# The last group of a scan-and-FFN kernel packed to 64 partitions and 256 columns, its gating named as an item of its own, and new slots for the work between scan steps

## The reference

```python
p = patches(x)                                   # (32, 196, 768)
y = layernorm(p, ln1_g, ln1_b) @ W + bias
h = concat([layernorm(y, ln2_g, ln2_b), txt])    # (32, 273, 256)

u = layernorm(h)[:, ::2]                         # every second token
u = u * rsqrt(mean(u * u) + eps) * g_norm
x, gate = split(u @ w_in.T + b_in)               # 256 each
def step(s, xt):                                 # s: (32, 256, 64)
    s = tanh(s * A + xt[:, :, None] * Bm)
    return s, s @ Cm.sum(0) + Dv * xt
out = scan(step, 0, x) * silu(gate)
h = h + repeat(out @ w_out.T + b_out, 2)[:, :273]

f = layernorm(h)
return h + (silu(f @ wg.T) * (f @ wu.T)) @ wd.T  # hidden 768, weights whole numbers / 127
```

## Time and profile before

| | |
|---|---|
| median of 3 runs | 1384.4 us (1383.81 to 1384.44) |
| profiled execution, own time | 1382.85 us |
| its span, first to last instruction | 1381.1 us |
| mean granted TensorE clock | 0.977 |
| busy PE / DVE / ACT / POOL | 1198.4 / 1089.9 / 989.5 / 430.9 us |
| scan slots | 1096 |

### The profile page before, as it was taken

How to read it: one execution, slowest core, us unless ns; L and a number is a source line. 1 busy time by engine, 2 the same in 40 slices (tenths; PEclk the granted TensorE clock), 3 DMA queues, 4 the chain that set the end, 5 groups by cost and what they waited for, 6 DMA issues and landing times.

```text
span 1381.1 us, 25884 instructions
## 1 busy us (share of the span) xinstructions
PE 1198.4 (87%) x7137; PEld 637.7 (46%) x7137; DVE 1089.9 (79%) x2423; ACT 989.5 (72%) x1944; POOL 430.9 (31%) x435
## 2 busy tenths in 40 slices
PE   4587889898989898989898989898999999998866
PEld 3343445354545454545454545454444444443433
DVE  4896878788888888788888788868888888887732
ACT  2367686868686868686868787878778888886632
POOL 6512151515151515151525151524121221221130
PEclk9689999999999999999999999999999999999997
DMA  7412323232323232323131414121323323323200
GB/s 161 126 36 62 74 61 87 61 85 61 85 61 85 61 85 61 85 58 88 53 93 49 97 45 101 40 67 49 100 68 86 86 67 87 85 51 84 55 20 15
DMA packets 154813, 99.59 MB, mean 72 GB/s; under 512 B 129072, under 2 KB 143536, under 8 KB 153424
## 3 DMA queue, kind: packets, MB, share of 16 engines
q1 hardware_dynamic: 151120, 97.58, 27.6%
q10 hardware_dynamic: 3648, 1.46, 0.5%
HBM read 58.39 MB, written 40.60 MB: 72 GB/s over the span
## 4 chain that ended last, share of the span: by engine, by line
PE 31%; issue 27%; ACT 10%; DVE 10%; POOL 9%; DMA 8%; SPq 4%; POOLq 0%; ACTq 0%; DVEq 0%
PE Y L1354 6%; PE U L1344 6%; PE P L1521 5%; PE P L1522 5%; ACT h L1076 4%; DVE U L814 4%; PE P L1455 3%; DMA yT<-y_scr 3%; ACT rawn L1092 3%; DMA y_scr<-y_fx 2%; DMA raw<-in_x 2%; SPq L688 1%; POOL yT L1238 1%; DVE raw_st L821 1%; POOL zT L1242 1%
## 5 line engine op out<-in xcount | busy, mean ns | idle before, releaser
L814 DVE TENSOR_TENSOR U<-h,a_col 128x512 f32<-128x512 f32 x1096 | 707.0, 689 | 128.5 <-ACT h L1076 125.5
L1076 ACT ACTIVATE h<-U 128x512 f32<-128x512 f32 x1096 | 605.8, 607 | 189.0 <-PE U L1344 188.2
L1344 PE MATMUL U<-x_diag,b_st 128*128 128x512 f16 x1096 | 369.3, 385 | 72.8 <-DVE U L814 64.3
L1354 PE MATMUL Y<-h,read_st 128*32 128x512 f32 x2192 | 265.6, 602 | 1.5 <-ACT h L1076 1.5
L1344 PEld LDWEIGHTS U<-x_diag,b_st 128*128 128x128 f16 x1096 | 103.7, 98 | 261.6 <-DVE U L814 182.0
L1279 POOL TENSOR_TENSOR xT_act<-act,xT_act 128x448 f16<-128x448 f32 x114 | 116.6, 1039 | 215.0 <-ACT xT_act L1173 215.0
L1420 PE MATMUL P<-tok_w,xT_act 128*112 128x256 f32 x648 | 159.5, 386 | 1.2 <-ACT xT_act L1100 0.9
L1420 PEld LDWEIGHTS P<-tok_w,xT_act 128*112 128x112 f32 x648 | 113.2, 178 | 42.6 <-issue 10.7
L1536 PE MATMUL P<-down_w,xT_act 128*112 128x256 bf16 x480 | 115.6, 279 | 5.4 <-POOL xT_act L1279 3.0
L1354 PEld LDWEIGHTS Y<-h,read_st 128*32 128x32 f32 x2192 | 57.5, 109 | 129.7 <-issue 120.1
L1537 PE MATMUL P<-down_w,xT_act 128*112 128x256 bf16 x480 | 114.7, 277 | 0.0
(11 more groups left out here) (159 smaller groups left out, 1441.6 us busy)
## 6 DMA issues: line engine op xcount, KB each, us to landing
raw<-in_x SPq DMA_DIRECT2D x42, 448.0 KB, 6.3
gate_scr<-gate_o SPq DMA_DIRECT2D x20, 448.0 KB, 2.5
gate_in<-gate_scr SPq DMA_DIRECT2D x20, 448.0 KB, 3.5
tok_scr<-tok SPq DMA_DIRECT2D x19, 448.0 KB, 3.1
res<-tok_scr SPq DMA_DIRECT2D x19, 448.0 KB, 3.8
out<-res SPq DMA_DIRECT2D x76, 112.0 KB, 5.1
x_diag<-scan_scr SPq DMA_DIRECT2D x312, 16.0 KB
x_diag<-scan_scr SPq DMA_DIRECT2D x304, 12.0 KB
```

The costliest lines, as they stand in the source:

```text
L814: dve.tensor_tensor(U[bank_of(slot)][:, :].rearrange("p (l b) -> p l b", b=B), h[:, (slot - CHUNKS) % RING, :].rearrange("p (l b) -> p l b ...
L1076: sc.activation(h[:, slot % RING, :], U[bank_of(slot)][:, :], ACT.Tanh, scale=1.0 / U_SCALE).then_inc(squashed, 1)
L1344: pe.matmul(U[bank_of(slot)][:, :], b_st[:, c, :], x_diag[:, c, :, t * B:t * B + B], start=False, stop=True, skip_group_check=True).then_i ...
L1354: mm = pe.matmul(Y[c4 * 32:c4 * 32 + 32, :], read_st[:, t, half, :], h[:, (t * CHUNKS + half * RG + c4) % RING, :], start=(t == 0 and half ...
```

## The change

1. Every table of `PLANS` and all of `POOL_ORDER` but "zero" have new numbers.
2. A function `rows_of(group)` gives 64 partitions (16 images x 4 steps) for the last group and 112 for the others. The attention's output, the turn of the FFN's input, its copies, FFN, silu, product, high and low parts, shrink and finish of the last group work on 64 partitions, 64 or 256 columns. Its x and gate copies are 128 columns where they were 224; the loads of its text tokens and its stores step over 4 where they stepped over 7.
3. The gating of the last group, an item of stage "tail", is now `gating_next` at the end of stage "last".

```diff
 PLANS = {
     "image": dict(
-        shrink=(2, 3, 3, 3, 5, 7, 7, 7), turn=(7, 9, 10, 12, 13, 14, 15, 15), attend=(17, 18), average=(20, 22),
-        embed=(19, 19, 19, 20, 20, 21, 24, 25, 26, 29, 29, 29), turn_fx=(30, 30), ffn_gate=(34, 37, 39, 45, 46, 48),
-        ffn_up=(34, 37, 44, 45, 49, 53), turn_xa=(36,), project=(39, 41, 46, 46), finish=(8, 10), raw_patch=(18, 18,
-        18, 18, 18, 18, 19, 19, 20, 22, 22, 22, 22, 22), raw_means=(23,), raw_deviation=(24,), raw_variance=(25,),
-        res_stats=(25,), res_variance=(26,), res_shift=(28,), fx_low_part=(34, 34), tok_stats=(29, 33),
...
-        ffn_silu=(34, 37, 42, 43, 45, 51), act_high_part=(40, 41, 43, 46, 48, 54), normalise=(55, 55, 55, 55, 55,
-        55, 55), residual=(23,)),
+        shrink=(1, 3, 3, 3, 4, 4, 5, 8), turn=(8, 10, 10, 12, 13, 15, 15, 16), attend=(17, 17), average=(20, 21),
+        embed=(18, 18, 18, 19, 20, 22, 24, 24, 24, 26, 29, 29), turn_fx=(30, 30), ffn_gate=(34, 37, 40, 44, 45, 47),
+        ffn_up=(34, 38, 43, 44, 49, 52), turn_xa=(36,), project=(40, 42, 46, 46), finish=(6, 10), raw_patch=(18, 18,
+        18, 18, 18, 19, 20, 20, 20, 20, 20, 20, 20, 20), raw_means=(21,), raw_deviation=(23,), raw_variance=(24,),
+        res_stats=(24,), res_variance=(24,), res_shift=(26,), fx_low_part=(34, 34), tok_stats=(27, 33),
...
+        ffn_silu=(33, 37, 41, 43, 44, 48), act_high_part=(37, 43, 44, 49, 49, 53), normalise=(52, 55, 55, 55, 55,
+        55, 55), residual=(20,)),
     "text": dict(
...
-        ffn_up=(37, 39, 46, 47, 48, 52), turn_xa=(27,), project=(30, 30, 31, 32), finish=(11, 21), res_stats=(30,),
-        res_variance=(31,), res_shift=(31,), fx_low_part=(36, 36), ln_stats=(22,), ln_shift=(25,), x_low_part=(33,),
...
+        ffn_up=(38, 39, 42, 46, 50, 52), turn_xa=(26,), project=(29, 30, 31, 31), finish=(14, 19), res_stats=(30,),
+        res_variance=(30,), res_shift=(31,), fx_low_part=(36, 36), ln_stats=(23,), ln_shift=(25,), x_low_part=(32,),
...
     "last": dict(
...
-        ffn_up=(42, 44, 48, 51, 55, 55), finish=(11, 16), res_stats=(27,), res_variance=(33,), res_shift=(38,),
-        fx_low_part=(46, 50), ffn_product=(55, 55, 55, 55, 55, 55), y_copy=(0,), fx_apply=(35, 38, 46, 48),
...
-        residual=(26,), y_next=(54,)),
...
+        ffn_up=(42, 46, 47, 50, 52, 55), finish=(19, 20), res_stats=(33,), res_variance=(37,), res_shift=(51,),
+        fx_low_part=(55, 55), ffn_product=(55, 55, 55, 55, 55, 55), y_copy=(6,), fx_apply=(32, 34, 35, 36),
...
+        residual=(33,), y_next=(49,)),
...
 POOL_ORDER = {
...
     "last": (
-        ("gating", 0), ("res_rsqrt", 0), ("act_low_part", 0), ("act_low_part", 1), ("act_low_part", 2),
-        ("act_low_part", 3), ("act_low_part", 4), ("skip_term", 0), ("act_low_part", 5)),
+        ("gating", 0), ("res_rsqrt", 0), ("act_low_part", 0), ("act_low_part", 1), ("skip_term", 0),
+        ("act_low_part", 2), ("act_low_part", 3), ("act_low_part", 4), ("act_low_part", 5), ("gating_next", 0)),
...
     "tail": (
-        ("gating", 0), ("res_rsqrt", 0)),
+        ("res_rsqrt", 0),),
...
+        def rows_of(group):
+
+            return 16 * LAST_STEPS if isinstance(group, int) and group == GROUPS - 1 else PT
...
             def ffn_product(k):
                 dve.wait_ge(ffn_u_ps, q * HB + k + 1)
                 dve.wait_ge(fsg_done, q * HB + k + 1)
-                dve.scalar_tensor_tensor(act[:, k, :], fsg[:, k % 2, :], ACT_SCALE * DEQUANT, up_bank(k, scan)[:, 0:4 * PT],
+                n = 4 * rows_of(q)
+                dve.scalar_tensor_tensor(act[:, k, 0:n], fsg[:, k % 2, 0:n], ACT_SCALE * DEQUANT, up_bank(k, scan)[:, 0:n],
                                          ALU.mult, ALU.mult).then_inc(act_done, 1)
...
-            def gating():
+            def gating(q):
...
-                gp.tensor_tensor(zT[:, :, :].rearrange("p k (b t) -> p k t b", t=STEPS),
-                                 y, gate_i[:, 1, :, :].rearrange("p k (t b) -> p k t b", b=B), ALU.mult).then_inc(z_done, 1)
+                n = rows_of(q) // 16
+                gp.tensor_tensor(zT[:, :, 0:B * n].rearrange("p k (b t) -> p k t b", t=n), y[:, :, 0:n, :],
+                                 gate_i[:, 1, :, 0:n * B].rearrange("p k (t b) -> p k t b", b=B), ALU.mult).then_inc(z_done, 1)
...
                 if post and name == "gating":
-                    gating()
+                    gating(q)
+                if post and name == "gating_next":
+                    gating(q + 1)
...
+                m = rows_of(q)
                 for j in range(DB):
-                    mm = pe.matmul(P[0][0:PT, k * D:k * D + D], zT[:, j, k * PT:k * PT + PT], out_w[:, j, :],
+                    mm = pe.matmul(P[0][0:m, k * D:k * D + D], zT[:, j, k * m:k * m + m], out_w[:, j, :],
...
-                bank = P[k // 2][0:PT, (k % 2) * D:(k % 2) * D + D]
+                m = rows_of(d)
+                bank = P[k // 2][0:m, (k % 2) * D:(k % 2) * D + D]
                 for f in range(f0, f0 + 3):
...
                         half = whole_part(down_w[:, f, :])
-                        pe.matmul(bank, act_hi[:, f, k * PT:k * PT + PT], half, start=(f == 0), stop=False)
-                        mm = pe.matmul(bank, act_lo[:, f, k * PT:k * PT + PT], half, start=False, stop=(f == HB - 1))
+                        pe.matmul(bank, act_hi[:, f, k * m:k * m + m], half, start=(f == 0), stop=False)
+                        mm = pe.matmul(bank, act_lo[:, f, k * m:k * m + m], half, start=False, stop=(f == HB - 1))
```

144 lines of the change are left out of this document (80 added, 64 removed).

## The result

The changed kernel takes 1377.28 us (median of 20 executions, 1372.27 to 1381.17), the kernel before 1385.06 beside it (20 executions, 1377.2 to 1388.89): a ratio of 0.9943, with a 95% interval of 0.9931 to 0.9955. It is faster, by 7.8 us where 15 to 16 were forecast; the time lies inside the range, the gain is half. The profiled execution has a span of 1376.0 us, 5.1 under that of the kernel before.

The account below looks back on a forecast made before the run. PE bounds the kernel on average (87% busy), with DVE saturated in part of the image stage and one chain at the end. Terms +1.6 + 0.4 - 6.0 - 3.6 - 7.9 = -15.5 us gave 1369 us as a median, range 1359 to 1382.

Parts of the forecast that it names:

- A: Start, up to the first drive: second half of normalised tokens computed later, first drive near 67.5; +1.6 us.
- B: First scanned stage: moved low part, spread bias splits, last POOL normalisation behind the skip term, delaying a raw load; +0.4 us.
- C: Twelve image stages: PE's 0.58 and ACT's 1.05 us waits vanish, second average costs 0.8; -0.5 us each, -6.0.
- D: Six text stages: residual variance directly follows its statistics, POOL's root runs under grow 30; -0.6 us each, -3.6.
- E: Last scan and the end: residual moved out of the scan and smaller last-group work; -7.9 us in all.
- e3: Last group, first turn to first FFN matmul: fewer columns shorten the rows on the chain; -1.1 us.
- e4: Last group's 48 FFN matmuls at 256 columns, lower clock for the first 5.6 us: 8.0 instead of 12.8; -4.8 us.
- e5: Last product with high and low part at 256 columns: 1.3 instead of 2.32 us; -1.0 us.
- e1: Last scan: residual and its statistics move behind the last grow, ACT's first apply starts sooner; -1.0 us.
- The steady stages do not move: Rival: image and text stages gain nothing because removed waits return as waits for saturated DVE; 1378.5 us, chance 0.20.
- the clock stays down: Rival: lower clock throughout last-group FFN and shrink, 5.4 us more, 1374.4; 1 in 10 of the forecast's chance.
- POOL's chain: Rival: later skip term delays gate's store and load, y's store and raw pixels, bounding the stage; 1393 us, chance 0.12.

Follow-up runs that it names:

- old_second: Changed kernel with table "second" and its POOL order as before the change: 1374.05 us (ratio 0.9912 to the kernel before).
- old_text: Changed kernel with the text table as before the change: 1370.2 us (ratio 0.9896 to the kernel before).
- no_pack: Changed kernel with the last group back at 112 partitions and 448 columns, slots as changed: 1379.54 us (ratio 0.9961 to the kernel before).
- image_avg22: Changed kernel with the image table's second average back at slot 22 instead of 21: 1372.82 us.
- image_tokn33: Changed kernel with ACT's second token normalisation in the image table back at slot 33 instead of 38: 1388.64 us (ratio 1.0032 to the kernel before).
- var30: Changed kernel with tables zero, first, second and text as before, except res_variance at slot 30 instead of 31: 1364.83 us.
- text_gate50: Changed kernel with the text stage's last gate matmuls at slot 50 instead of 52, fourth silu and product at 49: 1378.39 us (ratio 0.9965).
- pack_only: Kernel before with the packed last group only, all slot tables and POOL's order as before: 1376.23 us (ratio 0.9938 to the kernel before).
- old_start_text: Changed kernel with tables zero, first, second and text as before the change: 1364.87 us (ratio 0.9858 to the kernel before).

## Why the prediction was half right

**A and B, the start: +2.0 forecast, about +8 measured; the step that failed.** The working of A followed one path, xa, turn_xa, the first drive. turn_xa did come 2.9 us later (48.94 for 46.08). But the last eight projection matmuls, which took 3.3 us at the lower clock before, took 2.1 now, and the first drive came at 64.2, 1.6 earlier than before, not at 67.5. The first squash came when it had come before (66.45 for 66.47), because ACT now issued its loads in one block and normalised behind them. The price was paid in the scans: 3.9 us in that of group 0, 3.8 in that of group 1 and 0.6 in that of group 2, by the means above. Term B is what had them wrong. It named the bias splits and the last normalisation, priced the whole first scanned stage by the skip term, +0.4, because nothing of the scan waits for that directly, and gave the casts and the raw statistics that moved with it no price at all; the effect on the stage behind was put at nothing.

That the tables of the start as a whole carry the loss is shown. Which item does is open. Three were put back one by one and none shortened the first scan. Table "second" alone gave back about 1.6 us in the first scan and 1.9 in the next (old_second). With POOL's order of stage "first" put back as well, DVE's block ahead of the second grow ended at about 70 us all the same, once stretched, once held back. One part can be read, though nobody tested it alone: in the scan of group 1 DVE stood 3.4 to 3.8 us for the raw pixels in the changed kernel, old_text, no_pack and image_avg22, whose loads are issued 7 to 10 us behind the scan's first squash; with the old start it stood 1.7 to 3.1, the loads issued 5 to 7 us behind it. It is a delay of the kind that B named, the next raw load, and priced at 0.4.

**C, image stages: -0.5 a stage forecast, about -1.0 measured; right in sign, wrong in mechanism.** The prediction named the embedding's wait (0.58) and ACT's (1.05). Both went and brought nothing. The gain came from a move that it did not price: ACT's second token normalisation, from slot 33 to 38, behind the normalisation of xa, which took 1.14 us of PE's standing away. image_tokn33 gives the whole of it back. The second average made PE stand 1.3 us where 0.8 was forecast, and cost nothing in the end, which image_avg22 shows. The sentence that a wait removed beside the saturated DVE comes back as another was right, and should have been applied to both sides of the sum, the loss too.

**D, text stages: -0.6 a stage forecast, +0.7 measured in the four that can be compared; wrong.** POOL's root does run under a grow now, and DVE's wait fell by 0.62. PE's wait for DVE rose by 0.68 at the same place (var30). The sentence that the banks absorb in part what stands ahead of grow 30 was the error: the stage was as long as without the item, to 0.05 us, so all that DVE's wait lost came back. What the stage lost, 0.6 of 0.7, is in the shrink, two slots earlier; the prediction did not look at it.

**E, the last scan and the end: -7.9 forecast, -6.4 measured; the terms right together, the clock between them not foreseen.** (The scan of group 18, a text stage, was 2.0 shorter besides; it had 3.4 us at the lower clock for 6.8 before.) e3 was -1.1 and is -1.2 (3.70 to 2.54). e4 was -4.8 and is -5.6: the 48 matmuls took 6.9 us, the first 3.7 us of it at 1.2 GHz.

```profile
1353.33 0.37 PE L1547 MATMUL U<-fx_split,gate_w 128*128 128x256 f16 x1 [1.43 <-DVE fx_split L977]
...
1360.23 0.27 PE L1548 MATMUL Y<-fx_split,up_w 128*128 128x256 f16 x1
```

```profile
1353.34:1357.00 3.66, 3.66 (x18) 2.54 (x19) 0.48 (x2) 1.17 (x3) 0.00 (x0) 0.50 0.00 0
1357.00:1360.20 3.20, 3.20 (x31) 2.86 (x30) 2.10 (x6) 1.91 (x6) 0.00 (x0) 1.00 0.00 0
```

The spacings are those forecast, 0.213 and 0.109. The lower level held 17 to 18 of them, not 26. e5 was -1.0 and is -0.4. e1 was -1.0 and is -1.7: the scan ends 4.1 us earlier, the turn of group 18 comes 4.4 us behind it instead of 2.0. The shrink was 0 and is 0 (7.2 us both times, 3.4 of it at the lower clock). Those are -8.9. Then the changed kernel gives back 2.6 us between the turn of group 18 and the last group's: FFN of group 18 12.0 us for 11.2, its shrink 9.6 for 7.7. Most of it is the clock: no_pack, with the same rows there, takes 30.5 us from turn to turn, the changed kernel 32.7 and the kernel before 30.1. These are the first matmul of that shrink and the stretch at the lower clock:

```profile
1336.24 0.32 PE L1563 MATMUL P<-down_w,xT_act 128*112 128x256 bf16 x1 [2.52 <-POOL xT_act L1296]
```

```profile
1336.40:1339.90 3.50, 3.50 (x18) 3.46 (x18) 0.00 (x0) 0.00 (x0) 1.60 (x2) 0.52 0.00 0
```

PE had stood 2.5 us ahead of it, as in before (2.43), where the clock stayed up. All kernels with the new text table, whole or in most of its items, and the packed tail had that stretch, except text_gate50; pack_only, old_text, old_start_text, var30 and no_pack did not. This is where old_text got what it gained behind the last scan beyond its stages, 3.4 us: 2.0 between the two turns, and 1.6 in the last group's shrink, which ran wholly at the upper clock there (5.6 us for 7.2). That the clock's fall in that shrink depends on when the stage begins, and not on a wait that one could take away, is argued from this and not shown.

The prediction drew on a rule of the Trainium skill ("TensorE: Matmul & The Clock Gate", What's actually happening), that warm-up is a budget of time and not a number of matmuls. The last group's FFN had 16 matmuls of 448 columns in 5.7 us at the lower level before, 17 to 18 of 256 in 3.7 after. These two alone look like a number. no_pack, again at 448 columns, has 8 to 9 in 3.1:

```profile
1346.53:1349.60 3.07, 3.07 (x9) 1.30 (x10) 0.00 (x0) 0.54 (x1) 0.00 (x0) 0.50 0.00 0
1349.60:1356.93 7.33, 7.33 (x40) 3.75 (x39) 4.70 (x9) 4.39 (x9) 0.00 (x0) 1.00 0.00 0
```

So it is not a number, as that section of the Trainium skill says; and the time left of the low stretch when the FFN begins is not a constant either. The forecast took it for one (5.6 us, measured 3.7).

**The rivals.** "The steady stages do not move" gave 1378.5, near the measured time, for a wrong reason: they moved by -9.8 and +2.6, and the start took 10.6 (8.3 by the means). That the new slots lose elsewhere held for the start and the text stages. That the clock stays down held for 3.4 us of the shrink of group 18, not for the FFN and shrink of the last group. POOL's chain did not become the bound, but came close. These rows of the changed kernel are ACT's y copy and SP's two issues:

```profile
561.95 0.60 ACT L1086 ACTIVATE y_fx<-Y 128x512 f32<-128x512 f32 x1
```

```profile
561.68 0.37 SPq L681 DMA_DIRECT2D gate_in<-gate_scr  x1
562.78 2.21 SPq L688 DMA_DIRECT2D y_scr<-y_fx  x4
```

y's store is 0.83 us behind the start of y's copy, as before, and the gate's load was issued 1.1 ahead of it: of 7 us of slack 0.7 is left.
